# A post-norm attention and sparse feed-forward layer: order of the last scores and score banks, order of the first marks, and the tail by row tile

## The reference

```
x  = layernorm(x + attention(x))            # x: 4 batches x 512 rows x 512
x  = layernorm(x + ffn(x))                  # layernorm without weights, eps 1e-5
attention: q = x@wq (32 heads of 16), k = x@wk, v = x@wv (8 heads), softmax(q k^T / 4) v, then @wo
ffn:  inter = x @ c1^T @ c2^T               # rank 16, 1792 columns = 56 blocks of 32
      idx   = argmax of each block          # one column kept in each block
      h     = relu(x . w1[idx]);  out = sum of h * w2[idx]
```

## Time and profile before

| | us |
|---|---|
| median of 3 runs | 831.04 |
| the runs | 830.64, 831.04, 1455.67 |
| the profiled execution | 832.09 |
| its span, first to last instruction | 830.3 |

### The profile page before, as it was taken

How to read it: one execution, slowest core, us unless ns; L and a number is a source line. 1 busy time by engine, 2 the same in 40 slices (tenths; PEclk the granted TensorE clock), 3 DMA queues, 4 the chain that set the end, 5 groups by cost and what they waited for, 6 DMA issues and landing times.

```text
span 830.3 us, 11435 instructions
## 1 busy us (share of the span) xinstructions
PE 801.7 (97%) x4040; PEld 499.5 (60%) x4040; DVE 642.8 (77%) x827; ACT 387.0 (47%) x712; POOL 336.5 (41%) x444
## 2 busy tenths in 40 slices
PE   6999999999999999999999989999999999999994
PEld 5866433343333333333337768878878888788883
DVE  5588899999999999999216887878867887688763
ACT  4321688888888888888761321231311031112111
POOL 2212243753575455323411653433433343334441
PEclk9999999999999999999999989999999999999998
DMA  7684263344554454333406721240400030002001
GB/s 227 237 275 140 73 159 84 107 111 118 157 145 110 124 159 125 90 102 109 117 14 223 249 73 33 64 140 2 139 14 1 1 111 16 1 1 73 29 1 51
DMA packets 48192, 83.09 MB, mean 100 GB/s; under 512 B 9528, under 2 KB 13624, under 8 KB 48008
## 3 DMA queue, kind: packets, MB, share of 16 engines
q1 hardware_dynamic: 40448, 64.45, 25.5%
q0 software_dynamic: 7408, 16.81, 6.8%
q10 hardware_dynamic: 280, 1.11, 0.5%
HBM read 54.23 MB, written 28.05 MB: 99 GB/s over the span
## 4 chain that ended last, share of the span: by engine, by line
PE 86%; DVE 5%; ACT 4%; issue 2%; DMA 2%; SPq 0%; POOL 0%; ACTq 0%; POOLq 0%; DVEq 0%
PE ps_h L1246 18%; PE ps_pair L1263 18%; PE ps_pv L660 15%; PE ps_st L646 14%; PE ps_pair L633 6%; PE ps_st L608 6%; ACT probs L492 2%; PE ps_pv L608 2%; PE ps_pair L673 2%; ACT stage L463 1%; PE ps_prep L1223 1%; PE ps_prep L1218 1%; DVE neg_max L526 1%; PE ps_prep L1210 1%; DMA yf<-x 1%
## 5 line engine op out<-in xcount | busy, mean ns | idle before, releaser
L526 DVE TENSOR_REDUCE neg_max<-ps_pair 128x2 f32<-128x1024 f32 x256 | 301.4, 1219 | 30.6 <-PE ps_pair L633 30.6
L492 ACT ACTIVATE probs<-ps_st 128x512 f32<-128x512 f32 x512 | 266.3, 606 | 58.7 <-PE ps_st L646 57.7
L646 PE MATMUL ps_st<-q,k 50*128 50x512 f32 x512 | 185.1, 448 | 2.5 <-ACT probs L492 0.4
L646 PEld LDWEIGHTS ps_st<-q,k 50*128 50x128 f32 x512 | 83.3, 185 | 164.7 <-ACT probs L492 158.8
L982 ACT ACTIVATE g_h<-picked 128x512 fp32r<-128x512 f32 x56 | 35.5, 633 | 250.5 <-DVE picked L1100 250.5
L633 PE MATMUL ps_pair<-k,q 48*128 48x512 f32 x512 | 149.1, 440 | 1.8 <-DVE neg_max L526 1.8
L660 PE MATMUL ps_pv<-probs,v 128*32 128x512 f32 x1024 | 136.4, 605 | 0.0
L899 POOL TENSOR_TENSOR g_l<-picked,g_h 128x512 fp32r<-128x512 f32 x56 | 72.5, 1294 | 127.6 <-ACT g_h L982 127.6
L1246 PE MATMUL ps_h<-xt_h,w_h 128*128 128x512 f32 x224 | 90.6, 405 | 3.4 <-DVE picked L1100 3.4
L1246 PE MATMUL ps_h<-xt_h,w_l 128*128 128x512 f32 x224 | 89.8, 401 | 0.0
L1246 PE MATMUL ps_h<-xt_l,w_h 128*128 128x512 f32 x224 | 89.6, 400 | 0.0
(11 more groups left out here) (152 smaller groups left out, 1141.8 us busy)
## 6 DMA issues: line engine op xcount, KB each, us to landing
operands<-parts POOLq DMA_DIRECT2D x20, 512.0 KB, 3.6
q<-operands SPq DMA_DIRECT2D x64, 128.0 KB, 2.7
sums<-stage SPq DMA_DIRECT2D x32, 256.0 KB, 3.1
x_raw<-xT SPq DMA_DIRECT2D x16, 256.0 KB, 5.1
k<-operands SPq DMA_DIRECT2D x64, 64.0 KB, 2.3
q<-operands SPq DMA_DIRECT2D x64, 64.0 KB, 2.5
att<-sums SPq DMA_DIRECT2D x16, 256.0 KB
yf<-x SPq DMA_DIRECT2D x4, 1024.0 KB, 7.1
```

The costliest lines, as they stand in the source:

```text
L492: nc.scalar.activation(probs[kt % 2][:, r], ps_st[i % 3][:], ACT.Exp, scale=float(HD) ** -0.5).then_inc(exp_done, 1)
L526: nc.vector.tensor_reduce(neg_max[:, at:at + 2], ps_max[pair % 2][:], AX.X, ALU.max, negate=True).then_inc(max_red, 1)
L646: nc.tensor.matmul(ps_st[i % 3][:], k_[n % QR][64 * a:64 * a + ROWS, kt * P:(kt + 1) * P], q[n % QR][64 * a:64 * a + ROWS, j, :], start=Tr ...
```

## The change

**Last twelve attention steps.** `score_bank` gives the scores of the last three units (from score 464 on) five banks in turn: the three `ps_st` and the two halves of `ps_max[1]`. A score there waits for exponential i-5; the first score in each half of `ps_max[1]` waits until all row maxima are taken. The projection uses the two halves of `ps_max[0]` by turns, and tiles 2 and 3 wait for the residual sums of tiles 0 and 1. In these steps score 3 stands ahead of the weighing.

**First inner tiles.** VectorE's look is cut in two: `step` makes the transpose only, `first_in_block` the scan to the marks. In the slots 1 to 3 a slot first picks its own tile and then looks at tile i+1, not i+2. Slot 4 transposes tile 5 first, and looks at tiles 5 and 6 behind its pick. The residual sum of batch 2's row tile 3 goes ahead of the turning and pick of tile 1.

**Tail.** TensorE's last upward tile goes between the two halves of tile 53's contraction; the last two tiles are contracted by row tile in the order (54,0) (54,1) (55,0) (55,1) (54,2) (55,2) (54,3) (55,3). Tile 55's picks are split into the free buffers `xt_h[0]`, `xt_l[0]`, so they wait for no contraction. Statistics, variance and root are made for row tiles 0 to 2 first, then for row tile 3. ScalarE normalizes row tiles 0 and 1, VectorE 2 and 3, and SP waits for each by a semaphore of its own.

```diff
@@ _attend
+    WIDE = (NU - AHEAD) * TILES
+        def score_bank(i):
+            if i < WIDE:
+                return ps_st[i % 3]
+            return (ps_st[WIDE % 3], ps_st[(WIDE + 1) % 3], ps_max[1][:, 0], ps_max[1][:, 1], ps_st[(WIDE + 2) % 3]
+                    )[(i - WIDE) % 5]
...
-                nc.vector.tensor_tensor(y0[:, t], ps_max[t // 2][:, t % 2], y0[:, t], ALU.add).then_inc(added, 1)
+                nc.vector.tensor_tensor(y0[:, t], ps_max[0][:, t % 2], y0[:, t], ALU.add).then_inc(added, 1)
...
+                elif i < WIDE + 2:
+                    pe.wait_ge(exp_done, i - 2)
+                elif i < WIDE + 4:
+                    pe.wait_ge(max_red, NT // 2)
                 else:
-                    pe.wait_ge(exp_done, i - 2)
+                    pe.wait_ge(exp_done, i - 4)
...
+                if t >= 2 and third == 0:
+                    pe.wait_ge(added, t - 1)
...
                     scores_t(n, kt, 2)
+                    if n >= NU - AHEAD:
+                        scores_t(n, kt, 3)
                     if step:
                         weigh(*divmod(step - 1, TT))
-                    scores_t(n, kt, 3)
+                    if n < NU - AHEAD:
+                        scores_t(n, kt, 3)
@@ _feed_forward
+        row_ready = [sem(f"row_ready{t}") for t in range(TT)]
+        def picked_parts(i):
+            return (xt_h[0][:, 0], xt_l[0][:, 0]) if i == NB * MT - 1 else (g_h[i % 2][:], g_l[i % 2][:])
@@ SP
-                sp.wait_ge(out_ready, TT * (2 * NB - 1) + t + 1)
+                sp.wait_ge(row_ready[t], 1)
@@ GpSimd (ScalarE's high_g alike)
-                if i >= 2:
+                if 2 <= i < NB * MT - 1:
                     pool.wait_ge(out_mm, i - 1)
...
-            root(2 * NB - 1)
+            last, rows = 2 * NB - 1, slice(0, TT - 1)
+            pool.wait_ge(var_ready, last + 1)
+            pool.wait_ge(out_ready, TT * last)
+            nc.gpsimd.tensor_tensor(rstd[:, rows], var[:, rows], neg_half[:, rows], ALU.pow).then_inc(rstd_ready, 1)
+            pool.wait_ge(rstd_ready, last + 1)
+            nc.gpsimd.tensor_tensor(shift[:, rows], mv[:, rows, 0], rstd[:, rows], ALU.mult).then_inc(shift_ready, 1)
+            pool.wait_ge(shift_ready, 2 * last + 1)
+            nc.gpsimd.tensor_scalar(shift[:, rows], shift[:, rows], -1.0, None, ALU.mult).then_inc(shift_ready, 1)
+            pool.wait_ge(var_ready, last + 2)
+            nc.gpsimd.tensor_tensor(rstd[:, TT - 1:], var[:, TT - 1:], neg_half[:, TT - 1:], ALU.pow
+                                    ).then_inc(rstd_ready, 1)
@@ ScalarE
-            norm(2 * NB - 1)
+            act.wait_ge(shift_ready, 4 * NB)
+            for t in range(2):
+                nc.scalar.activation(y[0][:, t], y[0][:, t], ACT.Identity, bias=shift[:, t:t + 1],
+                                     scale=rstd[:, t:t + 1]).then_inc(row_ready[t], 1)
@@ VectorE
             front(marks(1))
+            first_in_block(1)
+            add_rows(2, 3)
             turn_marks(1)
             pick(0, 1)
-            add_rows(2, 3)
...
+                    if i == 4:
+                        step(0, marks(i + 1))
                     for following in steps:
...
                     if i >= 2:
                         pick(b, m)
+                    if 1 <= i <= 3:
+                        step(0, marks(i + 1))
+                    if 1 <= i <= 4:
+                        first_in_block(i + 1)
                     if 2 <= i + 1 < NB * MT:
                         turn_marks(i + 1)
-                    if i + 2 < NB * MT:
+                    if 4 <= i < NB * MT - 2:
                         step(*steps[-1])
+                        first_in_block(i + 2)
...
-            for t in range(TT):
...
-            variance(2 * NB - 1)
+            def last_norm(t, group):
+                dve.wait_ge(rstd_ready, last + group)
+                nc.vector.tensor_scalar(y[0][:, t], y[0][:, t], mv[:, t, 0:1], rstd[:, t:t + 1],
+                                        ALU.subtract, ALU.mult).then_inc(row_ready[t], 1)
+            for t in range(TT - 1):
+                last_sums(t)
+            dve.wait_ge(out_ready, TT * last)
+            last_variance(range(TT - 1))
+            last_sums(TT - 1)
+            last_variance(range(TT - 1, TT))
+            last_norm(TT - 2, 1)
+            last_norm(TT - 1, 2)
@@ TensorE
+                    if i == 0 or i == NB * MT - 1:
                         continue
...
                     inner_down(*before, (0, 1))
                     if i + 2 < NB * MT:
                         step(*steps[-1])
+                    else:
+                        inner_up(NB - 1, MT - 1, (0, 1, 2, 3))
                     inner_down(*before, (2, 3))
-            inner_down(NB - 1, MT - 1, (0, 1, 2, 3))
+            for m, t in ((2, 0), (2, 1), (1, 0), (1, 1), (2, 2), (1, 2), (2, 3), (1, 3)):
+                inner_down(NB - 1, MT - m, (t,))
```

More of the change, by code:

```diff
@@ L491, in _ @@
                             act.wait_ge(pv_done, n * TT + kt - 1)
-                        nc.scalar.activation(probs[kt % 2][:, r], ps_st[i % 3][:], ACT.Exp,
+                        nc.scalar.activation(probs[kt % 2][:, r], score_bank(i)[:], ACT.Exp,
                                              scale=float(HD) ** -0.5).then_inc(exp_done, 1)
@@ L670, in project_out @@
                     pe.wait_ge(att_split, REP)
+                if t >= 2 and third == 0:
+                    pe.wait_ge(added, t - 1)
                 for i in range(4 * third, 4 * third + 4):
                     r, (a, w) = i // 3, ((att_h, wo_h), (att_h, wo_l), (att_l, wo_h))[i % 3]
-                    last = nc.tensor.matmul(ps_max[t // 2][:, t % 2], a[0][:, r, t * P:(t + 1) * P], w[:, r],
+                    last = nc.tensor.matmul(ps_max[0][:, t % 2], a[0][:, r, t * P:(t + 1) * P], w[:, r],
                                             start=(i == 0), stop=(i == 11))
@@ L896, in low_g @@
                 pool.wait_ge(g_high, i + 1)
-                if i >= 2:
+                if 2 <= i < NB * MT - 1:
                     pool.wait_ge(out_mm, i - 1)
-                nc.gpsimd.tensor_tensor(g_l[m % 2][:], picked[m % 2][:], g_h[m % 2][:].bitcast(F32),
-                                        ALU.subtract).then_inc(g_ready, 1)
+                high, low = picked_parts(i)
+                nc.gpsimd.tensor_tensor(low, picked[m % 2][:], high.bitcast(F32), ALU.subtract).then_inc(g_ready, 1)
             def root(round_):
@@ L979, in high_g @@
                 act.wait_ge(picked_ready, i + 1)
-                if i >= 2:
+                if 2 <= i < NB * MT - 1:
                     act.wait_ge(out_mm, i - 1)
-                nc.scalar.activation(g_h[m % 2][:], picked[m % 2][:], ACT.Copy).then_inc(g_high, 1)
+                nc.scalar.activation(picked_parts(i)[0], picked[m % 2][:], ACT.Copy).then_inc(g_high, 1)
             def high_w2(m):
@@ L1151, in _ @@
             front(marks(0))
+            first_in_block(0)
             turn_marks(0)
@@ L1183, in _, with last_sums @@
                         variance(NB - 1)
-            dve.wait_ge(y_in[0], DMA * (NB + 1))
-            for t in range(TT):
+            last = 2 * NB - 1
+            def last_sums(t):
                 dve.wait_ge(last_mm, t + 1)
@@ L1189, in _, with last_variance @@
                 nc.vector.bn_stats(stats[:, t], y[0][:, t]).then_inc(stat_done, 1)
-            variance(2 * NB - 1)
+            def last_variance(tiles):
+                for t in tiles:
+                    dve.wait_ge(stat_done, TT * last + t + 1)
+                    nc.vector.bn_aggr(mv[:, t], stats[:, t]).then_inc(aggr_done, 1)
+                dve.wait_ge(aggr_done, TT * last + tiles[-1] + 1)
+                at = slice(tiles[0], tiles[-1] + 1)
+                nc.vector.tensor_scalar(var[:, at], mv[:, at, 1], EPS, None, ALU.add).then_inc(var_ready, 1)
+            def last_norm(t, group):
+                dve.wait_ge(rstd_ready, last + group)
+                nc.vector.tensor_scalar(y[0][:, t], y[0][:, t], mv[:, t, 0:1], rstd[:, t:t + 1],
+                                        ALU.subtract, ALU.mult).then_inc(row_ready[t], 1)
+            dve.wait_ge(y_in[0], DMA * (NB + 1))
+            for t in range(TT - 1):
[6 more added lines that the diff above has]
+            last_norm(TT - 1, 2)
         @block.tensor
@@ L1261, in inner_down @@
                         pe.wait_ge(added, TT * (NB - 2) + t + 1)
-                    for n, (g, w) in enumerate(((g_h, (w2_h, wo_h)), (g_h, (w2_l, wo_l)), (g_l, (w2_h, wo_h)))):
-                        last = nc.tensor.matmul(ps_out[t][:], g[m % 2][:, t * P:(t + 1) * P], w2_tile(*w, m),
+                    high, low = picked_parts(i)
+                    for n, (g, w) in enumerate(((high, (w2_h, wo_h)), (high, (w2_l, wo_l)), (low, (w2_h, wo_h)))):
+                        last = nc.tensor.matmul(ps_out[t][:], g[:, t * P:(t + 1) * P], w2_tile(*w, m),
```

45 lines of the change are left out of this document (23 added, 22 removed).

## The result

| | before, us | after, us |
|---|---|---|
| median | 830.84 | 817.00 |
| undisturbed executions | 828.11 to 831.04 | 816.66 to 818.15 |
| profiled execution | 832.09 | 818.15 |
| its span | 830.3 | 816.3 |

The medians are 13.8 us or 1.7% apart. The means of the undisturbed executions have the ratio 0.9847, 95% interval 0.9820 to 0.9873. The prediction was 817.5 us, range 814 to 822.5.

The account below looks back on a forecast made before the run. TensorE, busy for nearly the whole span, was taken as the bound. Gains of 4.3 + 5.4 + 3.9 = 13.6 us took the profiled 832.09 to 818.5; with the median 1.05 lower, 817.5 was named, range 814 to 822.5.

Parts of the forecast that it names:

- part C: Tail: first row tile complete sooner and norms shared between ScalarE and VectorE save 3.9 us, bounds 3.1 and 4.2.
- part B: First inner tiles: an earlier pick of tile 2 and a clock kept up save 5.4 us, bounds 4.7 and 5.9.
- A: Last twelve attention steps: a step falls from 3.20 to 2.77 us, saving 4.3 us, bounds -0.4 and 4.8.
- the change of shape is not saved: Rival, attention steps: the projection's first weight load waits out the weighing, saving -0.4 us there, time 822.1; chance 10%.
- Tile 2's marks meet the same GpSimd instructions: First inner tiles: these VectorE marks take 1.49 us while GpSimd's `xt_l` runs, so the pick starts at 480.0, not 483.12.
- one and a half waits: Ahead of tile 3's pick: VectorE's marks and variance wait for GpSimd, 1.05 us per wait; pick at 486.5, TensorE at 487.2.
- The work put off to slots 4 and 5: VectorE's postponed looks: 8.5 us between the picks of tiles 4 and 5, which just fits the 8.52 us there.
- the last transfer takes as long as now: Tail: the last output transfer was to take the same time as in the kernel before.
- the one worked out: Main case, whole kernel: the gains arrive as calculated, time 815.5 to 819.5; chance 59%.
- the fall of the clock: Rival, first inner tiles: the clock falls despite about 1.1 us idle, 2.6 us are not won, time 820.1; chance 12%.
- slower: Rival, whole kernel: slower than before, through TensorE's new wait for residual sum 0 if the load of `yf` lands late; chance 2%.
- over 2% faster: Rival, whole kernel: below 814.4 us, needing 16.6 us, more than all upper bounds together (14.9); chance 8%.

Follow-up runs that it names:

- e4: Changed kernel with score 3 behind the weighing again in the last twelve attention steps, five banks kept; 826.38 us in one execution.
- e12: The changed kernel itself, run again beside another kernel on the same chip; 817.35 us, ratio 0.9840.
- e1: Kernel before with only the change to the last twelve attention steps; 826.49 us against 830.87, ratio 0.9950.
- e7: Changed kernel with two very small VectorE memsets ahead of tile 2's look; 818.40 us in one execution.
- e10: Changed kernel with variance and root of the last four row tiles in three groups (rows 0 and 1, row 2, row 3); 816.59 us, ratio 0.9843.
- e6: Kernel before with twelve additional matmuls in TensorE's idle time ahead of inner tile 3; 829.94 us in one execution, against 830.75 beside it.
- e8: Changed kernel with tile 2's transpose made four times more, holding VectorE for 3.1 us; 821.68 us in one execution.
- e3: Kernel before with only the change to the tail; 827.79 us, ratio 0.9965.
- e9: Changed kernel with all four last row tiles normalized by ScalarE instead of two by VectorE; 816.93 us in one execution.

## Why the prediction was right, and where it wasn't

The time came out at 817.0 for 817.5. The mechanism of each part was right, but that the sum came so near is partly luck: part C was forecast too large, part B too small, and inside B two errors cancel.

- **A, 4.3 forecast, 4.2 in the trace, 4.4 timed alone.** Right in each step: the fourth score rides with the third, the change of shape into the full array costs no more than into a score, ScalarE is not late, the first step pays 0.44 us for the last maximum. The rival "the change of shape is not saved" falls. The wait for the residual sum of tile 0 never showed in the chain. One thing was left out: the new idle time of 1.08 us in the first step is a risk to the clock. It fell in the one trace of e4 behind the same wait, and in none of the seven traces that have this wait and the new order of scores (the changed kernel, e12, e1, e7 to e10). Whether the order of the scores or chance decides it was not tested.
- **B, 5.4 forecast, 5.8 timed alone (4.1 to 6.7), 7.1 or 5.8 in the traces.** The mechanism was right: the look of tile 3 out of the way, the idle time shortened, the clock kept (e6, e8). For the changed kernel the forecast was 487.2 - 461.43 = 25.8 us from mark product to tile 4, and it takes 24.2. One failed step is "Tile 2's marks meet the same GpSimd instructions". VectorE got there 0.05 us before GpSimd, 0.44 us instead of 1.49, and so TensorE had not even the 1.1 us of idle time forecast. With e7's 0.3 us of delay the step comes out as written: pick 18.60 us behind the mark product, idle time 1.06, clock 1.00. The other is the one and a half waits ahead of tile 3's pick: its marks took 0.79 us and the variance 0.17, so the pick (480.45) was ready before TensorE (481.61). The work put off to slots 4 and 5 fitted; TensorE waited for nothing there. For the kernel before, the forecast took its one trace, 31.3 us, where e1 and e3 have 30.0: the clock cost 1.3 us less in them. This error offset most of the other two in the timed gain.
- **C, 3.9 forecast, 3.0 in the trace, 3.1 timed alone.** The last row was ready sooner than forecast (7.7 us behind the first sum instead of 8.05; VectorE's norm took 0.54 us, not 0.69, GpSimd's second root 0.81, not 1.04). The failed step is "the last transfer takes as long as now". From the last row to the end it was 3.7 us, not 2.5. Four transfers of 256 KB take 0.70 us each, one behind another, and end 4.5 us behind the first issue. In the changed kernel the rows come faster than that, so only the first row's time counts. In the kernel before ScalarE's pitch of 0.74 us hid this, since it was about a transfer's own time, and the two bounds fell together. e9 shows it, and e10 the other bound: there the last row comes late enough to set the end.

The cases: the one worked out came true; of the rivals, the fall of the clock had a real mechanism, and its price was paid where the idle time was put back (e8) and in the first step of e4, but not in the changed kernel. The other sides (slower, or over 2% faster) lie outside the interval of 0.9820 to 0.9873.

## What to carry to other kernels

Count the changes of shape on TensorE in a repeated step: a small matmul that stands alone between two shapes paid 0.43 us here, and beside its partner nothing. When an idle time ahead of matmuls is removed, count the clock behind it too: here 1.6 us of 5.8 or 3.0 of 7.1, by the trace one takes. So look at more than one execution before such a term goes into a sum. And don't leave a new microsecond of waiting behind at another place. At the end of a kernel look at what the output transfers need in a row; where the results come faster than their transfers, the first one to be ready is worth more than the last.

## What the runs showed of the hardware

- The granted clock fell to 0.53 behind an idle time of 1.08 us in e4 and not behind the same 1.08 us in the changed kernel or 1.06 us in e7; in e8, with 2.3 us, it fell only some way into the work behind. The length of one idle time alone doesn't tell whether the clock falls.
- Nor does it tell the price: behind the same 3.40 to 3.44 us of idle time the way from tile 3 to tile 4 took 8.88 us in the kernel before and 7.58 and 7.55 in e1 and e3, where it takes 5.93 at a granted clock of 1.00.
- A bf16 `tensor_tensor` of VectorE took 0.44 us when it began 0.05 us ahead of a GpSimd instruction, 1.49 us when it began 0.09 us behind one (the kernel before), and 1.34 us when 0.25 behind (e7).
- GpSimd's power took 1.04 us for four columns, 0.88 for three, 0.73 for two and 0.57 for one; the one column took 0.79 to 0.81 us where VectorE's scalar operation on a 128x512 tile in SBUF ran beside it. VectorE's fp32 scalar operation of 128x512 took 0.54 us.
- Four 256 KB output DMAs from SP ended 4.5 us behind the first issue when they were issued within 2.04 us and 4.5 us behind it when within 2.44 (e9), with the DMA engines busy without a gap at 376 to 378 GB/s. Issued within 3.00 us (e10) they ended 5.1 us behind it.
